# Latent attention with a gated mixture on one Trainium2 core: the attention stage and the combination put into one block

## The chip, the cores and the metric

The kernel runs on one core of one Trainium2 chip. The metric is the device time of one launch in microseconds. Engines are TensorE (PE, PEld for its weight loads), VectorE (DVE), ScalarE (ACT), GpSimd (POOL) and SyncE (SP), which here only issues transfers.

## The reference

The input x has 2048 tokens of width 512. After a layer norm, two branches are computed and multiplied, and x is added:

```python
xn = _layernorm(x)
s = attention(xn)                      # 16 heads, head width 128, rotary width 64, latent width 128
g = silu(ffn(xn))                      # dense 512x512 plus 8 low-rank experts, two of them per token
out = x + s * g
# attention
c_Q = xn @ W_DQ.T;  q = [c_Q @ W_UQ.T , rope(c_Q @ W_QR.T)]
c_KV = xn @ W_DKV.T; k = [c_KV @ W_UK.T, rope(xn @ W_KR.T)];  v = c_KV @ W_UV.T
scores = clip(q @ k.T, -80, 80), causal; weights = softmax(scores / sqrt(192))
s = concat_heads(weights @ v) @ W_O.T
```

All is float32. The kernel splits each factor of a large matmul into a high and a low part (names ending in `_h` and `_l`) and adds three products.

## The kernel before

The kernel has three stages, each a block of its own in which every engine has its own program.

`prepare` normalises x, computes keys, values, latent queries and the linear branch, and stores them in memory (`keys`, `values`, `linear`, `turned`).

`attend` walks over 16 units (`UNITS`), a unit being 256 tokens (`CT`, a couple of tiles) for 8 of the 16 heads. A unit of couple m has 2m + 2 pairs. A pair is a block of 128 keys against the 256 tokens of the unit: the first is the CORNER (causal), the second LATE (only the later 128 tokens), the others FULL. `sweep` calls `pair` on every engine in the same order, 144 pairs in all (`PAIRS`), with hardware loops for the FULL pairs. In a pair TensorE computes scores in two halves (L916 to L928, L946), ScalarE takes the exponential (L1087), VectorE clips (L1177, L1182), ScalarE rounds to the high part (L1093), VectorE adds up the sums (L1190) and subtracts for the low part (L1195), and TensorE weighs the values of the pair before (L968, L987 to L991). Attention outputs stay unnormalised in the latent space; at the end of a unit ScalarE reads them out (L1064), ones times `total` gives the sums (L901), and GpSimd's queue stores both (L831, L833). It also gathers the next unit's rotated queries (L791, L794). SP's queue loads keys (L810) and values (L813) into two slots each.

In unit 15 the corner has no next unit, so no latent queries are computed. Two single transfers on GpSimd's queue bring the weights `wo` (L866, released at 1121.47 by the first half of the scores of unit 15's corner) and `uv` (L869). VectorE inverts the sums of units 0 to 13 in the second FULL pair's end (`early_sums`, L1233), and GpSimd's queue stores them (L871).

`combine` is the third block. TensorE computes the 16 products W_UV times W_O per head into `merge_ps` (L1365), ScalarE and VectorE split them (L1408, L1465), and for each of 16 tiles of 128 tokens the rows of all heads are loaded (L1308), the inverse sums are loaded onto one partition (L1313) and spread by GpSimd (`partition_broadcast`, L1358), VectorE multiplies (L1423), ScalarE takes the high part (L1391), VectorE the low (L1429), and TensorE does 48 matmuls into `sum_ps` (L1376 to L1378). The sigmoid (L1402), the gate product (L1441) and two operations in `finish` (L1447, L1449) follow. Buffers are doubled by the tile's parity. SP also stores the last unit's outputs and sums, loads the late sums (L1333), and stores their inverses (L1335).

The order on each engine is written out by hand with semaphores.

## Time and profile before

| | us |
|---|---|
| median of 3 runs | 1454.61 (1453.51 to 1456.13) |
| profiled execution, its own time | 1453.58 |
| its span, first to last instruction | 1452.1 |
| TensorE busy | 1378.6 (95%) |
| VectorE busy | 1141.7 (79%) |
| ScalarE busy | 781.3 (54%) |
| GpSimd busy | 112.6 (8%) |

The span is what the rows below are placed in; the profiled execution's own time is 1.5 us above its span. Matmul records overlap, so the pitch from start to start, not the duration, is what one costs. TensorE's granted clock averages 0.988 of full speed.

### The profile page before, as it was taken

How to read it: one execution, taken by the hardware profiler on the slowest of the kernel's cores; microseconds unless marked ns; L12 is line 12 of the kernel's file. 1: busy time of each engine (PE TensorE's matmuls, PEld its weight loads, DVE VectorE, ACT ScalarE, POOL GpSimd, SP SyncE). 2: the span in 40 equal slices, each digit the busy share in tenths (PEclk: the TensorE clock that was granted, in tenths of full speed). 3: DMA queues.
4: the chain of work that ended last, by engine and by line, in shares of the span. 5: the costliest groups of instructions: out<-in, count | busy, mean ns of one | idle time of the engine just before them, and what ended most of it. 6: DMA issues, size and time to landing. Idle time of an engine off the chain costs nothing. (4 is left out here: it accounts for less than half of the span.)

```text
span 1452.1 us, 27828 instructions
## 1 busy us (share of the span) xinstructions
PE 1378.6 (95%) x9808; PEld 1133.0 (78%) x9808; DVE 1141.7 (79%) x1322; ACT 781.3 (54%) x854; POOL 112.6 (8%) x150
## 2 busy tenths in 40 slices
PE   5999689999999999999999999999999799599998
PEld 5888567778778888888889888887788688278887
DVE  5666378888888898989888898888788598576764
ACT  3322367666666666666666665666556466332221
POOL 0000111101101101010010100100000000112121
PEclk9999899999999999999999999999999999899999
DMA  6422665535424424242251421422412522345562
GB/s 265 134 90 85 187 187 153 168 130 157 120 89 148 123 85 124 84 126 83 58 152 58 123 87 61 136 74 56 129 54 83 189 57 58 117 132 161 167 181 87
DMA packets 111949, 172.77 MB, mean 119 GB/s; under 512 B 9224, under 2 KB 68904, under 8 KB 109096
## 3 DMA queue, kind: packets, MB, share of 16 engines
q1 hardware_dynamic: 97528, 111.10, 24.8%
q0 software_dynamic: 13552, 59.60, 14.0%
q10 hardware_dynamic: 832, 1.57, 0.5%
q8 instruction: 22, 0.36, 0.1%
q14 instruction: 15, 0.12, 0.0%
HBM read 123.75 MB, written 48.50 MB: 119 GB/s over the span
## 5 line engine op out<-in xcount | busy, mean ns | idle before, releaser
L1093 ACT CAST prob_h<-prob 128x1024 fp32r<-128x1024 f32 (+1 forms) x288 | 289.7, 1006 | 230.4 <-DVE prob L1177 183.1
L946 PE MATMUL score_ps<-q_h,key_slot 64*128 64x512 f32 x1792 | 360.8, 394 | 14.7 <-DMA key_slot<-keys 14.5
L1087 ACT ACTIVATE prob<-score_ps 128x1024 f32<-128x1024 f32 (+1 forms) x288 | 281.8, 978 | 168.0 <-PE score_ps L946 119.0
L1195 DVE TENSOR_TENSOR prob_l<-prob,prob_h 128x1024 fp32r<-128x1024 f32 (+1 forms) x288 | 335.9, 1166 | 39.7 <-ACT prob_h L1093 38.2
L968 PE MATMUL out_ps<-prob_h,value_slot 64*128 64x512 f32 (+1 forms) x1792 | 341.5, 375 | 0.2
L1190 DVE TENSOR_TENSOR total<-total,prob 128x1024 f32<-128x1024 f32 (+1 forms) x256 | 294.9, 1152 | 0.0
L1177 DVE TENSOR_SCALAR prob<-prob 128x1024 f32<-128x1024 f32 x224 | 155.2, 693 | 84.8 <-ACT prob L1087 84.6
L946 PEld LDWEIGHTS score_ps<-q_h,key_slot 64*128 64x128 f32 x1792 | 173.8, 185 | 52.8 <-DMA key_slot<-keys 10.8
L968 PEld LDWEIGHTS out_ps<-prob_h,value_slot 64*128 64x128 f32 x1792 | 173.7, 185 | 33.6 <-DVE prob_l L1195 2.3
L946 PE MATMUL score_ps<-q_l,key_slot 64*128 64x512 f32 x896 | 179.0, 391 | 0.0
L946 PE MATMUL score_ps<-rot_hh,key_slot 64*128 64x512 f32 x896 | 178.9, 390 | 0.0
L968 PE MATMUL out_ps<-prob_l,value_slot 64*128 64x512 f32 (+1 forms) x896 | 172.3, 376 | 0.0
L1391 ACT CAST rows_h<-rows 128x1024 fp32r<-128x1024 f32 x32 | 33.7, 1053 | 128.6 <-DVE rows L1423 127.2
L1376 PE MATMUL sum_ps<-merged_h,rows_h 128*128 128x512 f32 x256 | 100.0, 391 | 0.0
L946 PEld LDWEIGHTS score_ps<-rot_hh,key_slot 64*128 64x128 f32 x896 | 86.7, 184 | 16.9
L1378 PE MATMUL sum_ps<-merged_h,rows_l 128*128 128x512 f32 x256 | 99.6, 389 | 0.0
L1377 PE MATMUL sum_ps<-merged_l,rows_h 128*128 128x512 f32 x256 | 99.6, 389 | 0.0
L968 PEld LDWEIGHTS out_ps<-prob_l,value_slot 64*128 64x128 f32 x896 | 86.9, 185 | 16.1
L946 PEld LDWEIGHTS score_ps<-q_l,key_slot 64*128 64x128 f32 x896 | 86.8, 185 | 12.8
L946 PE MATMUL score_ps<-rot_l,key_slot 64*128 64x512 f32 x448 | 89.4, 390 | 0.0
L1182 DVE SCALAR_TENSOR_TENSOR prob<-prob,causal 128x1024 f32<-128x1024 f32 (+1 forms) x64 | 61.1, 954 | 17.3 <-ACT prob L1087 16.9
L1423 DVE TENSOR_TENSOR rows<-rows,scale 128x1024 f32<-128x1024 f32 x32 | 39.5, 1271 | 31.2 <-POOL scale L1358 31.2
(192 smaller groups left out, 1979.9 us busy)
## 6 DMA issues: line engine op xcount, KB each, us to landing
key_slot<-keys SPq DMA_DIRECT2D x144, 256.0 KB, 2.7
value_slot<-values SPq DMA_DIRECT2D x144, 128.0 KB, 2.0
rows<-heads_rows SPq DMA_DIRECT2D x32, 512.0 KB, 5.8
rot_hh<-turned POOLq DMA_DIRECT2D x30, 512.0 KB, 6.0
heads_rows<-head_rows POOLq DMA_DIRECT2D x15, 1024.0 KB, 10.0
turned<-rot_hl POOLq DMA_DIRECT2D x14, 1024.0 KB, 4.6
rot_l<-turned POOLq DMA_DIRECT2D x30, 256.0 KB, 7.9
wo<-in_w_o POOLq DMA_DIRECT2D x1, 4096.0 KB, 14.5
```

The source lines that it names most:

```text
L946: mm = pe.matmul(score_ps[:, half, c * 512:(c + 1) * 512], keys_of[ROWS[r], :], moving[par][ROWS[r], half * HW + c * 512:half * HW + (c + ...
L968: mm = pe.matmul(out, values_of[ROWS[r], :], moving, start=False, stop=False)
L1087: nc.scalar.activation(prob[half][:, 0:width], score_ps[:, half, 0:width], ACT.Exp, scale=QK_SCALE).then_inc(exp_done, 1)
L1093: nc.scalar.copy(prob_h[half][:, 0:width], prob[half][:, 0:width]).then_inc(high_done, 1)
L1177: nc.vector.tensor_scalar(p, p, P_MIN, P_MAX, ALU.max, ALU.min).then_inc(clipped, 1)
L1182: nc.vector.scalar_tensor_tensor(out=heads, in0=heads, scalar=P_MIN, in1=limit, op0=ALU.max, op1=ALU.min).then_inc(clipped, 1)
L1190: nc.vector.tensor_tensor(sums, sums, by_head(half, kind), ALU.add).then_inc(summed, 1)
L1195: nc.vector.tensor_tensor(p_l, p, p_h, ALU.subtract).then_inc(split, 1)
L1376: pe.matmul(sum_ps[:, par, :], rows_h[par][:, h, :], merged_h[:, h, :], start=(h == 0), stop=False)
L1377: pe.matmul(sum_ps[:, par, :], rows_h[par][:, h, :], merged_l[:, h, :], start=False, stop=False)
L1378: mm = pe.matmul(sum_ps[:, par, :], rows_l[par][:, h, :], merged_h[:, h, :], start=False, stop=(h == HEADS - 1))
L1423: nc.vector.tensor_tensor(rows[par][:, heads, :], rows[par][:, heads, :], scale[par][:, heads, :], ALU.mult).then_inc(scaled, 1)
```

## The change

The blocks `attend` and `combine` become one block, `attend_and_combine`. To make the memory fit, `homes` places buffers of the combination where attention buffers lie whose last use is past. The same edits also move work:

- The weights are loaded in 20 parts by GpSimd's queue, each released by one half pair's scores in unit 13, instead of in two transfers in units 14 and 15.
- The 16 products per head and their split run in the corner pair of unit 15 (on TensorE where other units compute latent queries); the LATE pair's scores wait for the subtractions.
- The inversion of the early sums moves to the same corner, ahead of the split.
- GpSimd's queue, once all 16 products are split, loads rows of tiles 0 and 1 and their scales, the scales spread to all partitions by the transfer. Later tiles are spread by GpSimd as before.
- VectorE multiplies and splits tile 0 in the last four FULL pairs of unit 15 (`closes`), ScalarE copies in two of them; for that the last four pairs of the last couple's units stand outside the loop.
- After the sweep TensorE computes tile 0 (`project(0, 0)`), then the last two weighings and the last sums, then tile 1 and the others. Around it, SP, ScalarE and VectorE have a new order for the first tiles.

The core of the diff:

```diff
                 if not (isinstance(m, int) and m == 1):
-                    with eng.Fori(1, m) as n:
+                    with eng.Fori(1, m - 2 if closing else m) as n:
                         two(t + 2 + 2 * n, unit, 2 * n, FULL)
+                if closing:
+                    two(t + 2 * m - 2, unit, 2 * m - 4, FULL)
+                    two(t + 2 * m, unit, 2 * m - 2, FULL)
...
+        def closes(unit, kind, k, before):
+            return not unit.has_next and kind == FULL and isinstance(k, int) and k == 2 * unit.couple - before
...
             sweep(sp, pair)
+            sp.wait_ge(heads_stored, 16 * (UNITS - 2))
+            sp.wait_ge(inverses_out, 16)
+            load_rows(2, 0)
+            load_scale(2, 0)
+            sp.wait_ge(scored, 2 * PAIRS)
+            load_rest(0, 0)
+            load_rest(1, 1)
+            load_rows(3, 1)
+            load_scale(3, 1)
+            sp.wait_ge(out_read, 2 * UNITS)
+            sp.dma_start(one_of(heads_out, UNITS - 1), head_rows[:, :]).then_inc(last_stored, 16)
+            sp.wait_ge(sums_read, UNITS)
+            sp.dma_start(sums_out[UNITS - 1].rearrange("(q g) t -> q (g t)", g=2), sums[0:P:32, :]).then_inc(last_stored, 16)
...
+            sp.wait_ge(last_stored, 32)
+            sp.dma_start(late_sums, sums_out[EARLY:UNITS].rearrange("u h t -> (u h) t")).then_inc(late_in, 16)
+            for par in range(2):
+                load_rest(2 + par, par)
+                store(par, par)
+            sp.wait_ge(inverted, 2)
+            sp.dma_start(inverses[EARLY:UNITS].rearrange("u h t -> (u h) t"), late_sums).then_inc(late_out, 16)
+            with sp.Fori(1, COUPLES - 2) as n:
+                for par in range(2):
+                    tile(2 * n + par, par)
...
+            pool.wait_ge(passed, 16 * (UNITS - 2))
+            weights = [(wo[h], w_o[:, h, :]) for h in range(HEADS)]
+            for n in range(4):
+                columns = slice(n * 512, (n + 1) * 512)
+                weights.append((uv_flat[:, columns], w_uv[:, columns]))
+            for n, (home, source) in enumerate(weights):
+                pool.wait_ge(scored, 2 * (PAIRS - 4 * COUPLES - 2 * (COUPLES - 1) + 4) + n)
+                pool.dma_start(home, source).then_inc(weights_in, 16)
             during(UNITS - 2, 0, has_second=False)
...
-            pool.wait_ge(scored, 2 * (PAIRS - 2 * COUPLES) + 1)
-            pool.dma_start(top.wo[:, :, :], w_o).then_inc(weights_in, 16)
             during(UNITS - 1, 1, has_next=False, has_second=False)
-            pool.wait_ge(summed_up, UNITS - 1)
-            pool.dma_start(top.uv[:, :, :], w_uv.rearrange("p (h l) -> p h l", h=HEADS)).then_inc(weights_in, 16)
...
+            pool.wait_ge(merge_split, HEADS)
+            pool.wait_ge(summed_up, UNITS - 1)
+            pool.wait_ge(heads_stored, 16 * (UNITS - 2))
+            pool.wait_ge(inverses_out, 16)
+            for par in range(2):
+                for half in range(2):
+                    home, source = rows_of(par, par, half)
+                    pool.dma_start(home, source).then_inc(early_rows, 16)
+                pool.dma_start(scale[par], scale_of(par, par).partition_broadcast(P)).then_inc(early_rows, 16)
...
+                if kind == LATE and not unit.has_next:
+                    pe.wait_ge(merge_split, HEADS - 2)
...
+                        pe.wait_ge(weights_in, 16 * WEIGHT_PARTS)
+                        for h in range(HEADS):
+                            if h % 2 == 0 and h < 4:
+                                pe.wait_ge(exp_done, 2 * t + 1 + h // 2)
+                            since(pe, merge_split, h - 3)
+                            pe.matmul(merge_ps[h % 4], uv[:, h, :], wo[h], start=True, stop=True).then_inc(merged, 1)
...
             sweep(pe, pair)
+            pe.wait_ge(exp_done, 2 * PAIRS - 1)
+            project(0, 0)
             pe.wait_ge(values_in, 16 * PAIRS)
             for half in range(2):
                 weigh(PAIRS - 1, half, 1, FULL, True)
+            pe.wait_ge(summed, 2 * (PAIRS - UNITS))
+            sum_up(1, score_ps[:, 0, DIM:2 * DIM])
             pe.wait_ge(exp_done, 2 * PAIRS)
+            project(1, 1)
+            with pe.Fori(1, COUPLES) as n:
+                for par in range(2):
+                    pe.wait_ge(times[par], n)
+                    project(2 * n + par, par)
...
+                    if closes(unit, kind, k, 3):
+                        high_half(0, 0, 0)
+                    if closes(unit, kind, k, 2):
+                        high_half(0, 0, 1)
...
             sweep(act, pair)
+            high_rows(1, 1, 0)
+            high_rows(2, 0, 1)
             for half in range(2):
                 act.wait_ge(weighed, 2 * PAIRS - 1 + half)
                 read_out(UNITS - 1, half)
+            read_sums(UNITS - 1, score_ps[:, 0, DIM:2 * DIM])
+            gates(0, 0)
+            gates(1, 0)
+            gates(0, 1)
+            high_rows(3, 1, 1)
+            gates(1, 1)
...
+                if closes(unit, kind, k, 4):
+                    dve.wait_ge(early_rows, 16 * EARLY_TILES)
+                    scale_half(0, 0)
+                if closes(unit, kind, k, 3):
+                    scale_half(0, 1)
+                if closes(unit, kind, k, 2):
+                    split_half(0, 0, 0)
+                if closes(unit, kind, k, 1):
+                    split_half(0, 0, 1)
...
+            scale_rows(1, 1, 0)
+            scale_rows(2, 0, 1)
             gates(0, 0)
+            gates(1, 1)
+            finish(0, 0, 0)
+            gates(2, 0)
+            finish(1, 1, 0)
+            dve.wait_ge(late_in, 16)
+            nc.vector.reciprocal(late_sums, late_sums).then_inc(inverted, 1)
```

## Rows read from the trace of the kernel before

**Rows 1.** The page's 40 slices, TensorE's busy tenths.

```profile
PE   5999689999999999999999999999999799599998
```

**Rows 2.** Windows: stretch, its length, busy time of each engine, clock, DMA share, GB/s.

```profile
1140.30:1145.60 5.30, 5.28 (x30) 4.44 (x32) 0.00 (x0) 0.39 (x1) 0.00 (x0) 0.50 0.29 84
1230.60:1237.40 6.80, 6.80 (x62) 5.43 (x58) 6.07 (x7) 4.16 (x5) 0.00 (x0) 1.00 0.07 19
1237.40:1273.95 36.55, 20.55 (x55) 9.26 (x54) 19.12 (x22) 14.83 (x22) 4.48 (x2) 0.81 0.38 117
1273.95:1448.07 174.12, 174.12 (x768) 143.79 (x767) 110.34 (x111) 42.66 (x48) 33.67 (x14) 1.00 0.51 150
```

**Rows 3.** Chain that ended last, between attention and combination: start, length, what.

```profile
1250.59 6.06 DMA scale<-inverses
...
1256.91 1.97 issue
1258.88 2.31 POOL scale L1358
...
1261.29 3.01 DVE rows L1423
...
1264.96 8.99 PE merge_ps L1365 x16
```

**Rows 4.** Timeline of TensorE at the borders of units 14 and 15: start, length, instruction, idle before.

```profile
1027.74 0.50 PE L946 MATMUL score_ps<-q_h,key_slot 64*128 64x512 f32 x2 [1.15 <-DMA key_slot<-keys]
...
1126.08 1.06 PE L901 MATMUL out_ps<-total,ones 128*32 128x512 f32 x8
1128.78 0.47 PE L987 MATMUL out_ps<-prob_h,value_slot 128*128 128x512 f32 x1 [1.63 <-issue]
...
1140.32 0.80 PE L946 MATMUL score_ps<-q_h,key_slot 64*128 64x512 f32 x2 [6.23 <-DMA key_slot<-keys]
```

**Rows 5.** Timeline of ScalarE between attention and combination.

```profile
1245.90 0.58 ACT L1408 CAST merged_h<-merge_ps 128x512 fp32r<-128x512 f32 x1 [1.45 <-PE merge_ps L1365]
1246.76 0.58 ACT L1408 CAST merged_h<-merge_ps 128x512 fp32r<-128x512 f32 x1 [0.27 <-PE merge_ps L1365]
...
1274.59 1.28 ACT L1402 ACT_TABLE_LOAD   x1
```

**Rows 6.** Timeline of VectorE: unit 15's corner, its second full pair, last pair, a tile.

```profile
1128.23 1.23 DVE L1195 TENSOR_TENSOR prob_l<-prob,prob_h 128x1024 fp32r<-128x1024 f32 x1 [1.11 <-ACT prob_h L1093]
...
1158.87 1.75 DVE L1233 RECIPROCAL early_sums<-early_sums 112x256 f32<-112x256 f32 x1
...
1238.06 0.69 DVE L1177 TENSOR_SCALAR prob<-prob 128x1024 f32<-128x1024 f32 x1 [0.27 <-ACT prob L1087]
...
1241.01 1.22 DVE L1190 TENSOR_TENSOR total<-total,prob 128x1024 f32<-128x1024 f32 x1
...
1289.90 2.36 DVE L1423 TENSOR_TENSOR rows<-rows,scale 128x1024 f32<-128x1024 f32 x2 [3.58 <-POOL scale L1358]
1292.25 2.36 DVE L1429 TENSOR_TENSOR rows_l<-rows,rows_h 128x1024 fp32r<-128x1024 f32 x2
```

**Rows 7.** Transfers: KB, median us to landing; landing of keys 1100 to 1160; SP's issues.

```profile
rows<-heads_rows SPq DMA_DIRECT2D x32, 512.0 KB, 5.8
heads_rows<-head_rows POOLq DMA_DIRECT2D x15, 1024.0 KB, 10.0
rot_l<-turned POOLq DMA_DIRECT2D x30, 256.0 KB, 7.9
wo<-in_w_o POOLq DMA_DIRECT2D x1, 4096.0 KB, 14.5
...
DMA to landing us min/median/max: 2.6/2.8/13.7
...
1224.91 0.33 SPq L810 DMA_DIRECT2D key_slot<-keys  x1
...
1280.73 1.42 SPq L1308 DMA_DIRECT2D rows<-heads_rows  x2
```

More of the change, by code:

```diff
@@ L73, in raw, with homes @@
     return ap.bitcast(F32)
+WO_FIRST = 13
+def homes(nc, ctx, side, words, sets):
+    made = []
+    for tensors in sets:
+        with ExitStack() as lent:
+            made.append([lent.enter_context(nc.sbuf_tensor(name, [P, width], dt, side=side)) for name, width, dt in tensors])
+    ctx.enter_context(nc.sbuf_tensor("home_of_" + sets[0][0][0], [P, words], F32, side=side))
+    return made
 class Persistent:
@@ L747, in attend, with by_heads @@
         out_ps = ctx.enter_context(nc.psum_tensor("out_ps", [P, 4, 512], F32))
+        def by_heads(ap, width):
+            return ap.rearrange("p (h n) -> p h n", n=width)
+        wo_parts = [by_heads(keep.wo_first[:, :], DIM), by_heads(wo_rest[:, :], DIM)]
+        wo = [wo_parts[h // WO_FIRST][:, h % WO_FIRST, :] for h in range(HEADS)]
+        uv = by_heads(uv_flat[:, :], LAT)
+        merged_h, merged_l = by_heads(keep.merged_h[:, :], DIM), by_heads(top.merged_l[:, :], DIM)
+        rows, scale, rows_h, rows_l = ([by_heads(ap[:, :], P) for ap in pair] for pair in (
+            (top.rows, rows1), (keep.scale, scale1), (keep.rows_h, rows_h1), (keep.rows_l, rows_l1)))
+        x_in, lin_in, gate = ([ap[:, :] for ap in pair] for pair in (
+            (keep.x_in, keep.x_in1), (lin_in0, lin_in1), (gate0, gate1)))
+        late_sums = late_sums[0:(UNITS - EARLY) * UHEADS, :]
+        result = [sb(f"result{n}", [P, DIM]) for n in range(2)]
+        merge_ps = [score_ps[:, b // 2, (b % 2) * DIM:(b % 2 + 1) * DIM] for b in range(4)]
+        sum_ps = [score_ps[:, par, 0:DIM] for par in range(2)]
         zeroed = sem("zeroed")
@@ L821, in _ @@
+            for par in range(2):
+                store(TILES - 2 + par, par)
+            for par in range(2):
+                sp.wait_ge(stored[par], 16 * COUPLES)
         @block.gpsimd
@@ L1127, in pair, with high_half, high_rows, gates @@
                     latent_high(n + 1, 1 - par, 1)
+                else:
+                    for h in range(HEADS):
+                        act.wait_ge(merged, h + 1)
+                        nc.scalar.copy(merged_h[:, h, :], merge_ps[h % 4]).then_inc(merge_high, 1)
                 begin(1)
+            def high_half(t, par, half):
+                heads = slice(half * UHEADS, (half + 1) * UHEADS)
+                act.wait_ge(scaled, 2 * t + half + 1)
+                nc.scalar.copy(rows_h[par][:, heads, :], rows[par][:, heads, :]).then_inc(rows_high, 1)
+            def high_rows(t, par, n):
+                since(act, projected[par], n)
+                for half in range(2):
+                    high_half(t, par, half)
+            def gates(par, n):
+                act.wait_ge(gate_in[par], 32 * (n + 1))
+                since(act, times[par], n)
+                nc.scalar.activation(gate[par], lin_in[par], ACT.Sigmoid).then_inc(sigmoid, 1)
             gather(act, 0, 0, first_scattered)
@@ L1230, in pair @@
                         split_turned(n)
-                if not unit.has_next and kind == FULL and isinstance(k, int) and k == 1:
-                    dve.wait_ge(early_in, 16)
-                    nc.vector.reciprocal(early_sums[:, :], early_sums[:, :]).then_inc(inverted, 1)
             latent_low(0, 0, 0)
```

331 lines of the change are left out of this document (127 added, 204 removed).

## The prediction

> **What bounds the kernel now.** I read the page first, then the windows by stage, then the chain of waits, and only then single engines around the one weak place. The slices of the page show TensorE at nine tenths or more nearly everywhere, with a visible dent in slice 34 and a small one in slice 31 [rows 1]. The windows say the same in numbers: in one attention pair (1230.6 to 1237.4) TensorE is busy 6.80 of 6.80 us, and in the whole combination (1273.95 to 1448.07) 174.12 of 174.12 us at a granted clock of 1.00 [rows 2]. So in both stages the sum of matmuls sets the time, and nothing but fewer idle stretches of TensorE can be gained.
>
> Between the stages the stretch from 1237.40 to 1273.95 holds 20.55 us of TensorE in 36.55 us [rows 2]. The chain shows what ends late there: a load of the inverse sums (6.06 us), a start of GpSimd (1.97), its broadcast (2.31), VectorE's scaling of tile 0 (3.01), then the rest of the products W_UV times W_O (8.99) [rows 3]. The dent in slice 31 is a load: TensorE sits idle 6.23 us at 1140.32 for a tile of keys [rows 4]. That load took up to 13.7 us instead of 2.8 [rows 7], while the single 4096 KB load of W_O (14.5 us) was under way, and the matmuls that follow run at clock 0.50, which is the 1.2 GHz level [rows 2].
>
> **The change, part by part.** The sum is made on the profiled execution, 1453.58 us in all with a span of 1452.1; the median of the three runs, 1454.61, is 1.0 above it.
>
> 1. The gap closes. After the last pair of the sweep (1237.40) the new order on TensorE is tile 0, the last weighing, the sums, tile 1, and so on. A tile is 174.12 / 16 = 10.88 us [rows 2]. What must still run between 1237.40 and the tiles is two weighings, 12 matmuls at a pitch of 0.23 us = 2.8 us, and the sums, 1.06 us [rows 4]: 3.9 us, the 0.23 being a tile's 10.88 / 48. Before, this stretch took 36.55 us until the first tile. Term: 3.9 - 36.55 = -32.6 us. It holds only if tiles 0 and 1 are prepared in time. Tile 1 is: VectorE's last addition, at 1241.01, ends at 1242.2, and its four operations of a tile take from 1289.90 to 1294.6 in steady state, ScalarE's copies among them, 4.7 us [rows 6], so tile 1 is ready near 1247 and needed at 1237.4 + 10.9 + 3.9 = 1252.2.
>
> 2. The 16 products move into the corner pair of the last unit. They are float32 matmuls, two instructions each, and the pitch of ScalarE's copies, 1245.90 to 1246.76, gives 0.86 us a head [rows 5]. In the old corner the sums start at 1126.08, last 1.06, and TensorE then idles 1.63 us until 1128.78 [rows 4]. New: the first four heads fill the four banks at 1127.15 + 3.4 = 1130.6; head 4 waits for VectorE, which finishes its piece of the pair at 1128.23 + 1.23 = 1129.46, now does the reciprocal (1.75 us [rows 6]) and then the first subtraction, 0.7 us, so 1131.9; twelve more heads, 12 x 0.86 = 10.3, end at 1142.4. The pair goes on there instead of at 1128.78. Term: +13.6 us. Bounds: 12.2 if the wait on VectorE costs nothing (16 x 0.86 - 1.6), 17 if copies and subtractions don't keep the pitch at first. All other work of the corner (ScalarE's 1.0 us copies) lies beside it. The scores after it wait for subtractions 14 and 16, whose last ones end within about 1.5 us of the products, and a weighing of 1.4 us and the first half's scores stand between: nothing.
>
> 3. The weights in 20 parts. 16 parts of 256 KB and 4 of 256 KB, one for each half pair (3.4 us), end before the corner of unit 14. A 256 KB load of keys takes 2.8 us [rows 7], so a part lands within its half pair, and pieces of 2 KB don't stand in front of the keys as rows of 32 KB did. GpSimd's queue waits on each part; behind it stands only the gather for unit 15, released later than the last part. Term: the stall of 6.2 us goes, and with it the low clock: 5.30 us at 0.50 [rows 2] would be 5.30 / 2 = 2.65 at 1.00. -6.2 - 2.6 = -8.8 us. The 1024 KB store of unit 14's rows stays where it is; it and the gathers cost a wait of 1.15 us at the border before [rows 4].
>
> 4. VectorE prepares tile 0 in the last four pairs: two multiplications and two subtractions, about 1.16 us each beyond overlap; ScalarE gets two copies of 1.05. In a pair VectorE is busy 6.07 of 6.80 us [rows 2], so 0.73 is free. Three of the four lie where TensorE still waits for VectorE (the last comes after the last subtraction of the sweep): 3 x 1.16 = 3.5, less the slack of two following pairs (1.5) and about 0.55 that TensorE's weighing lags: +1.5 us. Bounds 0 and 3.5. ScalarE has 4.16 of 6.80 busy [rows 2], so its copies hide. The last subtraction ends near 1243 to 1244 and TensorE wants it for the second half of tile 0 at 1242.9: within the same bounds.
>
> 5. GpSimd's queue loads tiles 0 and 1: four loads of 512 KB and two scales spread over 128 partitions by the DMA itself (1024 KB each). The trace of before has no such spread load. Rows of 512 KB take 5.8 us on SP's queue [rows 7] in 1024 pieces of 512 bytes; a scale has 2048 such pieces, so 11.6. Sum one after another: 4 x 5.8 + 2 x 11.6 = 46 us. Below lies 14.5 us, which W_O's 4096 KB took, above 126 us, by the 256 KB in 7.9 us of the rotated queries on the same queue [rows 7]; those were four loads side by side, so I stay at 46. They start after the 16th subtraction (1143.2) and VectorE wants them in the pair that begins 10 pairs after the late one: 1147.8 + 10 x 6.8 + 6 = 1222, 79 us later. Hidden. Meanwhile they share the engines with the keys, whose load is issued at 1224.91 for a pair that starts at 1230.60, with 5.7 us for 2.8 [rows 7]; I take +1 us in all, 0 to 6.
>
> 6. The start of the combination. Tile 2 reuses the buffers of tile 0, so SP issues it at about 1243.3 (last subtraction of tile 0). In steady state it is 9.2 us from SP's issue (1280.73) to VectorE's multiplication (1289.90) [rows 6, 7]; with up to 2 us for GpSimd's first broadcast, as in the chain [rows 3], tile 2 is multiplied from 1252.5 to 1254.5. ScalarE then copies its two halves (2.2), reads the last outputs and sums (2.6), loads a table (1.28 [rows 5]) and does two sigmoids; VectorE's two gate products and the first product of finish follow. That ends between 1262.3 and 1265.3, and TensorE asks for it (times[0]) at 1263.1: 0 to 2.2 us, I take 1.5. Then late_in: the store of the last rows is issued near 1260, takes 6 to 10 us (1024 KB, median 10.0 [rows 7]), the late sums and reciprocal follow, and the multiplication of tile 3 is queued behind that reciprocal on VectorE; ready at 1275 to 1278.5, needed at 1275.5: 0 to 3, I take 1.5. Tile 4's load is queued behind `inverted` on SP; it just meets its need. Term: +3 us, bounds 0 and 7.
>
> Sum: -32.6 + 13.6 - 8.8 + 1.5 + 1 + 3 = -22.3 us. 1453.6 - 22.3 = 1431.3; by the median of the runs 1432.3. I say 1431.5. No chance of no gain comes out of the terms themselves: +17, +3.5, +6 and +7 all at their bad ends give -32.6 + 17 - 8.8 + 3.5 + 6 + 7 = -7.9 us, 1445.7.
>
> **Rivals.** (a) The first tiles never wait: terms 4 and 6 at their good ends, -4.5 us, 1427 or a little under. For it: the links of the chain in 6 are worth 0 at their short ends. Against: three queues (ScalarE, VectorE, SP) each hold a late link. (b) The chain of the sums takes over: late_in on VectorE holds tile 3, `inverted` on SP holds tile 4, and with a 10 us store and the bad ends of 4 this is +4 to +7: 1436 to 1440. (c) The keys again: the many 512-byte pieces of the six loads hold up the keys of six or seven pairs by 1 to 1.5 us each: 1437 to 1441. For it is the 13.7 us load; against it that the neighbour there had rows of 32 KB. (d) The split does nothing, and some other transfer (the 1024 KB store) made the 13.7 us: term 3 is lost, 1440. Against: the same store at the border before costs 1.15 us [rows 4].
>
> (e) The other side: the six loads are late. VectorE stands at the wait for them ahead of the multiplication in the eleventh full pair, every later piece of attention is queued behind it, and TensorE stops. At the upper bound, 126 us against 79, it is 47 us: 1478. The point from which the kernel is slower is 79 + 22 + 3 = 104 us for the six. For it: descriptors of that queue are made by GpSimd. A mechanism that would do it: VectorE's clip works on 128x1024 in 0.69 us, where its additions need 1.22 [rows 6], and while it runs GpSimd may be shut out; twice 0.69 in 6.80 us is a fifth of the time, which stretches 46 to 58 us and stays under 79. The Trainium skill has this as a rule (SBUF — State Buffer, section on the "DVE blocks DMA" trap): in a two-port mode VectorE holds a port pair alone and GpSimd can't write the descriptors of its transfers. By that rule the loads belong on SP's queue. No row of before shows work held up by it.
>
> **How the numbers follow.** My forecast, 1427 to 1436, has 0.50; (a) under 1427 0.15; (b) 0.16; (c) 0.10; (d) 0.04; (e) 0.05. A measurement of this kernel tells about 0.2%, 3 us. The range 1424 to 1441 takes in (a) to (d) with the bounds of 4, 5 and 6. Faster 0.94, same 0.01, slower 0.05.
>
> **What would show it.** In the profile after: no stretch without TensorE between attention and combination, so slice dents at 31 and 34 gone and one of lower matmul density in the last unit's corner; merge_ps matmuls over some 15 us there at clock 1.00; key loads in the last unit within 5.7 us; early loads landed within about 46 us; waits of sum_ps on VectorE's result of 1 to 2 us at tile 2, and on rows_l at tile 3. It would be wrong if the corner costs more than 17 us, if sum_ps waits more than 7 us in all, or if VectorE's first scaling waits for a DMA.

## The result, and the profile after

The changed kernel takes 1446.45 us (median of 6 runs, 1444.91 to 1448.86) against 1454.06 for the kernel before (6 runs): ratio 0.9955, interval 0.9942 to 0.9967. It is faster, by 7.6 us where 22.3 were forecast, and its time lies 5 us above the range. The profiled execution took 1448.86 us with a span of 1447.4.

The page of the changed kernel, its 40 slices, numbered from 0: the dents in slices 31 and 34 [rows 1] are gone, but slice 35 holds a new one, and the clock has a dent there beside the one early on. A stall around 1158 us lies across slices 31 and 32 and doesn't show.

```profile
PE   4999689999999999999999999999999999979998
...
PEclk9999899999999999999999999999999999989999
```

TensorE's waits, 1000 to 1310 us: what waited and for whom, us in total, times, the longest. One wait of 8.1 us ahead of tile 2 and one of 4.6 us for keys make up most of what is missing from the forecast gain.

```profile
PE score_ps L1218 <- DVE result L1501: 8.1, 1, 8.1
PE score_ps L1103 <- DMA key_slot<-keys: 5.2, 2, 4.6
PE score_ps L1202 <- DVE merged_l L1465: 0.9, 1, 0.9
```

Windows (columns as in [rows 2]): the stall for keys and the stretch behind it, the last pair, the first two tiles with the last weighings and sums between them, the wait ahead of tile 2 and what follows it, and a stretch inside the combination.

```profile
1155.70:1160.30 4.60, 0.02 (x4) 0.01 (x2) 3.94 (x4) 1.77 (x2) 0.00 (x0) 1.00 1.01 372
1160.30:1165.00 4.70, 4.70 (x28) 3.71 (x30) 0.00 (x0) 0.05 (x1) 0.00 (x0) 0.64 0.75 281
1243.90:1250.70 6.80, 6.80 (x60) 6.07 (x56) 6.80 (x8) 4.84 (x5) 0.00 (x0) 1.00 0.08 23
1250.70:1277.20 26.50, 26.50 (x118) 20.33 (x116) 14.53 (x13) 4.51 (x5) 4.48 (x2) 1.00 0.39 119
1277.20:1285.30 8.10, 0.03 (x1) 0.00 (x0) 5.07 (x7) 6.51 (x8) 0.00 (x0) 0.70 0.32 130
1285.30:1291.00 5.70, 5.67 (x14) 4.45 (x15) 1.46 (x3) 0.63 (x1) 0.00 (x0) 0.53 0.50 144
1380.00:1400.00 20.00, 20.00 (x88) 16.27 (x87) 13.88 (x14) 5.48 (x6) 2.30 (x1) 1.00 0.62 184
```

Where 36.55 us held 20.55 of TensorE [rows 2], 26.50 are now full. Both stalls are dearer than they look: after each, the matmuls run for some us for a part at the lower clock level, 1.2 GHz (0.64 and 0.53 in the mean of the windows). In the last stretch 88 matmuls stand where the kernel before has 90 in the same 20 us.

TensorE's timeline in the last unit's corner and at the borders (start, length, instruction, idle before):

```profile
1128.63 1.07 PE L1058 MATMUL out_ps<-total,ones 128*32 128x512 f32 x8
1129.62 3.70 PE L1202 MATMUL score_ps<-wo_first,uv 128*128 128x512 f32 x8
1134.27 7.99 PE L1202 MATMUL score_ps<-wo_first,uv 128*128 128x512 f32 x18 [0.94 <-DVE merged_l L1465]
1142.10 2.74 PE L1202 MATMUL score_ps<-wo_rest,uv 128*128 128x512 f32 x6
1144.27 0.80 PE L1144 MATMUL out_ps<-prob_h,value_slot 128*128 128x512 f32 x1
...
1285.33 0.79 PE L1218 MATMUL score_ps<-merged_h,rows_h 128*128 128x512 f32 x1 [8.11 <-DVE result L1501]
```

The trace files `merge_ps` and `sum_ps` under `score_ps`, which holds them all now, so L1202 is the products and L1218 to L1220 are the tiles. From the sums to the next weighing it is 15.64 us, against 2.70 in [rows 4].

The wait ahead of tile 2, followed back. First VectorE and ScalarE:

```profile
1273.78 4.15 DVE L1419 TENSOR_TENSOR rows<-rows,scale 128x1024 f32<-128x1024 f32 x2 [11.97 <-POOL scale L1009]
...
1283.29 1.29 DVE L1495 TENSOR_TENSOR gate<-gate,lin_in 128x512 f32<-128x512 f32 x2 [2.97 <-ACT gate L1337]
1284.50 0.68 DVE L1501 TENSOR_TENSOR result<-score_ps,gate 128x512 f32<-128x512 f32 x1
```

```profile
1276.88 2.13 ACT L1326 CAST rows_h<-rows 128x1024 fp32r<-128x1024 f32 x2 [16.33 <-DVE rows L1419]
1278.91 1.92 ACT L1249 COPY head_rows<-out_ps 128x1024 f32<-128x1024 f32 x2
1280.72 0.60 ACT L1256 COPY sums<-score_ps 128x512 f32<-128x512 f32 x1
1281.34 1.28 ACT L1337 ACT_TABLE_LOAD   x1
```

Then GpSimd's broadcast by its line, with the marks of its sequencer; the first mark of a pass of the loop stands where the broadcast is released, in later passes 0.1 us ahead of its start (count, duration, first and last start):

```profile
L1009 POOLq MODIFY_POOL_CONFIG  x14: 11/11/11, 1263.1 to 1409.7; - x14
L1009 POOL PARTITION_BROADCAST scale<-scale x14: 2297/2297/2509, 1271.4 to 1421.1; - x14
```

The scale was there and the broadcast released at 1263.1; it began at 1271.4, 8.3 us later. Of the others, 12 begin when their scale lands and one right behind the first. VectorE had stood 11.97 us, and its two multiplications then took 4.15 us instead of 2.36, while GpSimd was spreading the second scale. The kernel before has the same start: the marks of its first broadcast are at 1252.3 and 1258.9, so 6.6 us. Its chain shows only 1.97 us of "issue" [rows 3]: the chain merges the first two broadcasts and follows the load of the second scale, which covers most of the start.

### The profile page after: what moved, and what is told of

Read it like the earlier page. It is cut to its first block, busy times and chain, and to the rows that moved or that the text cites. A ratio compares the mean times of both kernels' runs of the same rounds, so it can differ in the third digit from the quotient of the medians.

```text
span 1447.4 us, 27577 instructions
## 1 busy us (share of the span) xinstructions
PE 1384.2 (96%) x9808; PEld 1135.4 (78%) x9808; DVE 1143.9 (79%) x1322; ACT 780.9 (54%) x854; POOL 122.2 (8%) x172
## 4 chain that ended last, share of the span: by engine, by line
PE 74%; DMA 6%; DVE 5%; ACT 1%; issue 1%; SPq 0%; POOL 0%; POOLq 0%; DVEq 0%; ACTq 0%
PE score_ps L1103 29%; PE out_ps L1125 18%; DMA key_slot<-keys 5%; PE score_ps L1219 4%; PE score_ps L1218 4%; PE score_ps L1220 4%; PE out_ps L1144 2%; PE out_ps L1145 2%; PE out_ps L1148 2%; PE score_ps L1073 1%; PE score_ps L1074 1%; PE score_ps L1075 1%; PE score_ps L1076 1%; DVE prob_l L1415 1%; PE score_ps L1038 1%
## 5 line engine op out<-in xcount | busy, mean ns | idle before, releaser
L1103 PE MATMUL score_ps<-q_h,key_slot 64*128 64x512 f32 x1792 | 360.5, 393 | 10.8 <-DMA key_slot<-keys 10.7
L1218 PE MATMUL score_ps<-merged_h,rows_h 128*128 128x512 f32 x256 | 102.0, 399 | 8.1 <-DVE result L1501 8.1
L1219 PE MATMUL score_ps<-merged_l,rows_h 128*128 128x512 f32 x256 | 102.0, 399 | 0.0
L1220 PE MATMUL score_ps<-merged_h,rows_l 128*128 128x512 f32 x256 | 101.3, 396 | 0.0
L1218 PEld LDWEIGHTS score_ps<-merged_h,rows_h 128*128 128x128 f32 x256 | 48.9, 191 | 21.3 <-issue 9.7
```

Source lines behind the costliest of these rows:

```text
L1103: mm = pe.matmul(score_ps[:, half, c * 512:(c + 1) * 512], keys_of[ROWS[r], :], moving[par][ROWS[r], half * HW + c * 512:half * HW + (c + ...
L1218: pe.matmul(sum_ps[par], rows_h[par][:, h, :], merged_h[:, h, :], start=(h == 0), stop=False)
L1219: pe.matmul(sum_ps[par], rows_h[par][:, h, :], merged_l[:, h, :], start=False, stop=False)
L1220: mm = pe.matmul(sum_ps[par], rows_l[par][:, h, :], merged_h[:, h, :], start=False, stop=(h == HEADS - 1))
```

## The experiments

My theory after the result: the first broadcast of the program starts some 8 us late and is 8 of the missing us (with the low clock behind it 10.7); the burst of six loads makes the 4.6 us for keys. Rivals: the order on ScalarE (tile 2's copies ahead of the gates) makes the late sigmoid anyway; the keys are late by the place of their own slot, not by the burst; the 256 KB parts are not what cured the weights; and the place of buffers, or of the PSUM banks, or the clock, makes the slower pitch. Kernels that were not timed side by side are compared by their ratios to the kernel before, times 1453 us, the others by their medians; an interval of such a ratio is some 2 us to either side.

**First broadcast early.** GpSimd does one small broadcast of its own after the six loads.

```diff
+            nc.gpsimd.memset(ready_tile[:, :], 0.0).then_inc(ready, 1)
+            pool.wait_ge(ready, 1)
+            nc.gpsimd.partition_broadcast(ready_tile[:, :], ready_tile[0:1, :], channels=P).then_inc(ready, 1)
+            pool.wait_ge(ready, 2)
```

> The changed kernel, and GpSimd runs one partition broadcast of 8 elements right after it has issued the six early loads, about 115 us before the first real one. Theory (the first broadcast on GpSimd takes about 8 us from its release to its start, and this makes tile 2 late): the first real broadcast starts under 1 us after its scale has landed, TensorE's wait of 8.1 us ahead of tile 2 falls to 0 to 2 us and the low clock behind it goes with it, so 8 to 11 us less than the changed kernel: ratio to the kernel before 0.987 to 0.990. Rival 1 (the wait for the scale's transfer or for the loop of the queue sets the start): the start stays 8 us after landing, ratio 0.9955. Rival 2 (ScalarE's order of read-outs and gates sets tile 2): the broadcast comes early, but the wait stays over 5 us.

1437.74 us, ratio 0.9893 (0.9877 to 0.9909), 9 us under the changed kernel. GpSimd's timeline:

```profile
1161.98 0.28 POOL L1026 PARTITION_BROADCAST ready_tile<-ready_tile  x1 [9.43 <-issue]
1264.29 2.30 POOL L1011 PARTITION_BROADCAST scale<-scale  x1 [102.03 <-DMA scale<-inverses]
1269.82 2.65 POOL L1011 PARTITION_BROADCAST scale<-scale  x1 [3.23 <-DMA scale<-inverses]
```

An instruction of 0.28 us began 9.3 us after its release (mark at 1152.7); the one of 2.30 us began when its scale landed. TensorE has no wait ahead of tile 2, and its wait for keys is unchanged at 5.1.

**Loads paced.** Each of the six loads waits for one more pair of unit 15.

```diff
+            for n, (home, source) in enumerate(early):
+                pool.wait_ge(scored, 2 * (PAIRS - 2 * COUPLES + 3 + n) + 1)
+                pool.dma_start(home, source).then_inc(early_rows, 16)
```

> The changed kernel, but each of the six early loads on GpSimd's queue waits for the first half scores of one further full pair instead of all going out at once. Theory (the burst of six loads, 4 MB, holds up the keys of the second full pair: landing 9.9 us instead of 2.7): no key load in the last unit over 5.5 us, no wait of TensorE there, and the stretch at low clock behind it gone: 5 to 6 us less than the changed kernel, ratio 0.9915 to 0.992. Rival (any single load of 512-byte pieces holds keys up, whatever is queued behind it): several key loads of 4 to 6 us, several waits of 1 us, and nothing gained. Rival 2: the instructions unrolled in the last unit cause the wait: it stays at 4.6 us.

1439.53 us, 0.9912 (0.9894 to 0.9930), 6 us under the changed kernel. TensorE waits 0.9 us for keys, and tile 2 still waits:

```profile
PE score_ps L1220 <- DVE result L1503: 7.4, 1, 7.4
PE score_ps L1105 <- DMA key_slot<-keys: 0.9, 1, 0.9
```

So the two waits are independent, and the burst is what made the second.

**Early scales spread by GpSimd.** The scales go to one partition, ahead of the rows, and are spread by two broadcasts, which both halves the bytes of the burst and moves the first broadcast.

```diff
-                pool.dma_start(scale[par], scale_of(par, par).partition_broadcast(P)).then_inc(early_rows, 16)
+                pool.dma_start(scale[par][0:1, :, :], scale_of(par, par).unsqueeze(0)).then_inc(early_scale, 16)
...
+            pool.wait_ge(early_scale, 32)
+            for par in range(2):
+                nc.gpsimd.partition_broadcast(scale[par], scale[par][0:1, :, :], channels=P).then_inc(early_spread, 1)
```

> The changed kernel, but the scales of tiles 0 and 1 are loaded onto one partition (8 KB each) and spread by GpSimd's broadcast in the last unit, as for the other tiles; four loads of 512 KB remain on the queue. It removes 2 MB of the 4 MB burst and moves the first broadcast far ahead of tile 2. Theory: both waits shrink. Ahead of tile 2 0 to 2 us instead of 8.1; the key load lands after 6 to 7 us instead of 9.9, so a wait of 1 to 2 us instead of 4.6. Together 11 to 14 us less than the changed kernel: 0.985 to 0.988. If the two broadcasts hold VectorE up in the last unit, up to 2 us of it is lost. Rival (size of the burst does not matter, one packet of the other queue in front of each packet does): the wait for keys stays at 4 to 5 us.

1435.51 us, 0.9888 (0.9871 to 0.9905), 10 us under the changed kernel where 11 to 14 were expected. TensorE waits 2.8 us for keys and 0.6 ahead of tile 2. With 2 MB of rows instead of 4 MB in all, the worst key load took 8.1 us instead of 9.9.

**Gates before tile 2.** ScalarE's and VectorE's work on tile 2 moves behind the gates of tiles 0 and 1; the broadcast stays as late as it was.

```diff
-            high_rows(2, 0, 1)
             for half in range(2):
...
             gates(1, 0)
+            high_rows(2, 0, 1)
             gates(0, 1)
```

> The changed kernel with another order in the hand-over: ScalarE reads the last outputs and sums and computes the gates of tiles 0 and 1 before it copies tile 2, and VectorE finishes tile 0 before it multiplies tile 2. Nothing else is changed, the first broadcast stays late. Theory: tile 2 then waits only for its own rows, which are ready near 3 to 4 us after TensorE has ended tile 1; the wait falls from 8.1 to 3 to 4 us, and the clock loss behind it to under 2: 5 us less, ratio 0.992. Rival (the chain through result and gates is only named last and the rows are as late): wait 7 us or more, ratio 0.995.

1438.31 us, 0.9905 (0.9889 to 0.9920), 7 us under, with a wait of only 1.0 on `rows_l` where I had expected 3 to 4. The late start is the cause, but it needs the order to do harm: in the changed kernel the sigmoid of tile 0 is queued behind the copies of tile 2. Here the first product of `finish` ends at 1266.8, 7 us before TensorE has done with tile 1, and tile 2's own rows, though the broadcast still began 7.1 us after its release, are only 1.0 us late.

**The kernel before with the weights in parts**, released by the scores of unit 15's pairs; nothing else changed.

```diff
+            for n, (home, source) in enumerate(parts):
+                pool.wait_ge(scored, 2 * (PAIRS - 2 * COUPLES) + 4 + n)
+                pool.dma_start(home, source).then_inc(weights_in, 16)
```

> The kernel before, with one part of the change alone: the weights in 20 parts of 256 KB, each released by one more half pair of the last unit; blocks, products and tiles stay as before. Theory (the 13.7 us key load was held up by the single 4096 KB load with its 32 KB rows): the wait of 6.2 us at the first full pair of the last unit goes, and the 2.6 us of low clock behind it, 8.8 us less: ratio 0.994. Rival (the 1024 KB store of the last outputs and the border itself hold the keys up): ratio 0.999 to 1, key landing still over 8 us.

1445.52 against 1454.14 on the same chip, 0.9951 (0.9937 to 0.9966): -8.6 us, where the term said -8.8. TensorE waits 0.9 us in all for keys instead of 6.2 and 1.2 [rows 4], and the gap before the combination is much as it was (12.3 us of waiting for `merged_l`, 13.1 before). The first part is issued at 1133.45, where the single load was at 1121.47, so this shows what the whole term is worth and not what the size alone is.

**Weights in three loads**, at the same place in unit 13 of the changed kernel.

```diff
+            weights = [(wo_parts[0], w_o[:, 0:WO_FIRST, :]), (wo_parts[1], w_o[:, WO_FIRST:HEADS, :]), (uv_flat[:, :], w_uv)]
...
+                pool.wait_ge(scored, 2 * (PAIRS - 4 * COUPLES - 2 * (COUPLES - 1) + 4) + 6 * n)
```

> The changed kernel with the weights in three transfers (3328, 768 and 1024 KB) in place of 20, from the same point on, 20 us apart. Theory (long rows on the other queue hold up keys): a key load of 10 us or more in unit 13 and a wait of 3 to 8 us of TensorE with a stretch of low clock, 5 to 9 us more than the changed kernel: ratio 0.999 to 1.002. Rival (in the middle of a unit keys have enough time): no wait over 1 us, ratio 0.9955 or a little less.

1448.03 us, 0.9961 (0.9946 to 0.9976), 1 to 3 us over the changed kernel's two ratios (0.9955 and, further down, 0.9943) and not clear of them, where 5 to 9 were expected. The dump of 3328 KB took 10.8 us and the worst key load beside it 7.2, which cost TensorE 1.5 us:

```profile
PE score_ps L1100 <- DMA key_slot<-keys: 1.6, 2, 1.5
```

So the place is worth most of the 8.8 us. It isn't that keys have more slack in mid-unit: a landing of 7.2 us left a wait of 1.5 there, so 5.7 were covered, and 13.7 left 6.2 in the kernel before, so 7.5 were. The delay itself was shorter. In the kernel before the store of unit 14's rows (1024 KB) and `uv` (1024 KB) were under way together with the 4096 KB; which of them made the difference was not tried.

**Three remedies together**: scales spread by GpSimd, the four row loads paced, and the early reciprocal behind the 16 subtractions instead of ahead of them.

```diff
-                        dve.wait_ge(early_in, 16)
-                        nc.vector.reciprocal(early_sums[:, :], early_sums[:, :]).then_inc(inverted, 1)
                         for h in range(HEADS):
...
+                        dve.wait_ge(early_in, 16)
+                        nc.vector.reciprocal(early_sums[:, :], early_sums[:, :]).then_inc(inverted, 1)
```

> The changed kernel with the scales of tiles 0 and 1 loaded onto one partition and spread by GpSimd, the four early row loads one per full pair, and the inversion of the early sums after the 16 subtractions in place of before them. Theory: no wait of TensorE over 1 us is left in the last unit nor ahead of tile 2, and the corner is 0.9 us shorter. 5.9 + 11.0 + 0.9 us less than the changed kernel, less up to 2 us for VectorE held up by the broadcasts: 16 to 18 us, ratio 0.983 to 0.985. Rival (a new late link takes the place of those removed, as tile 3 behind the late sums): ratio 0.987 to 0.989 with a wait of 3 us or more ahead of tile 3 or 4.

1431.64 us, 0.9854 (0.9840 to 0.9868), 15 us under the changed kernel. The waits on keys are down to 0.7 and those ahead of tiles are gone, but a new one stands in the pairs. VectorE's timeline while GpSimd spreads two scales in attention:

```profile
1153.64 1.22 DVE L1414 TENSOR_TENSOR total<-total,prob 128x1024 f32<-128x1024 f32 x1
1154.84 3.12 DVE L1419 TENSOR_TENSOR prob_l<-prob,prob_h 128x1024 fp32r<-128x1024 f32 x1
1157.88 2.78 DVE L1401 TENSOR_SCALAR prob<-prob 128x1024 f32<-128x1024 f32 x1
1160.59 1.21 DVE L1414 TENSOR_TENSOR total<-total,prob 128x1024 f32<-128x1024 f32 x1
```

1.2 and 0.69 us became 3.12 and 2.78, and TensorE waited 2.5 us.

**Tile 0 prepared after the sweep**: the multiplications, copies and subtractions of tile 0 leave the last four pairs.

```diff
-                if closes(unit, kind, k, 4):
-                    dve.wait_ge(early_rows, 16 * EARLY_TILES)
-                    scale_half(0, 0)
...
+            dve.wait_ge(early_rows, 16 * EARLY_TILES)
+            for half in range(2):
+                scale_half(0, half)
+            for half in range(2):
+                split_half(0, 0, half)
             scale_rows(1, 1, 0)
```

> The changed kernel without VectorE's part: tile 0 is multiplied and split after the last addition of attention, not in the last four pairs; ScalarE's two copies move too. Theory (the gap between the stages closes only because tile 0 is ready at the end of the sweep): TensorE waits 6 to 8 us ahead of tile 0, tile 2's loads start later too, so its wait stays near 8 us; the pairs are under 1 us faster. 7 to 10 us more than the changed kernel: ratio 1.000 to 1.003. Rival (tile 0's late start is taken back by a shorter wait ahead of tile 2): ratio 0.9955 to 0.998.

1447.83 us, 0.9962 (0.9948 to 0.9976): only 1 to 3 us over the changed kernel's two ratios, where 7 to 10 were expected. The waits show why:

```profile
PE score_ps L1218 <- DVE rows_l L1423: 9.5, 2, 8.2
...
PE score_ps L1218 <- DVE result L1490: 0.2, 1, 0.2
```

The wait moved from tile 2 to tile 0: the first broadcast began at 1271.21, as late as in the changed kernel, so TensorE did its idling earlier and asked for tile 2 later.

**The same with the three remedies in place.**

> The kernel of e7 (scales of tiles 0 and 1 spread by GpSimd, row loads paced, inversion after the subtractions), but tile 0 is multiplied and split after the last addition, as in e8. Theory (in e8 nothing was lost because the late tile 2 took the wait over; with the first broadcast early it no longer does): TensorE waits about 8 us ahead of tile 0 and loses 2 to 3 us at low clock, 8 to 10 us more than e7: ratio 0.991 to 0.992. Rival (preparing tile 0 in the last pairs is worth nothing in itself): ratio 0.986, wait under 3 us.

1441.58 us, 0.9921 (0.9906 to 0.9937). Against 0.9854 this is 10 us: tile 0 waits 8.2 us for `rows_l` and nothing comes back later. VectorE's part of the change is worth 10 us, and in the changed kernel the late broadcast takes most of it.

**The kernel before with the first broadcast early**, the same four lines as in the first experiment, at the head of the combination.

> The kernel before with one addition: at the start of the combination's program GpSimd runs one partition broadcast of 8 elements, while the loads of tile 0 are on their way. Theory (the first broadcast's 6.6 us from release to start is a cost of its being the first): the broadcast of tile 0 starts within 1 us of its scale's landing, and the chain up to tile 0 is 5 to 7 us shorter: ratio 0.9955 to 0.9965. Rival (the scale's transfer or the second scale's landing is what it waits for): start unchanged, ratio 0.999 to 1.001.

1447.49 against 1453.13 on the same chip, 0.9959 (0.9944 to 0.9974): -5.6 us. The single wait of TensorE among the first products, for `merged_l`, is 4.9 us instead of 13.1.

```profile
1250.86 0.28 POOL L1355 PARTITION_BROADCAST ready_tile<-ready_tile  x1 [7.02 <-issue]
1251.53 2.30 POOL L1364 PARTITION_BROADCAST scale<-scale  x1 [0.39 <-POOL ready_tile L1355]
```

The release mark is at 1244.0, 6.9 us ahead of the small broadcast. The late start was in the kernel before, too, and the chain had shown 1.97 us of it.

**All remedies without a broadcast in the way**: first broadcast early on the small tile, all six loads paced and spread by the transfer, reciprocal behind the subtractions.

> The changed kernel with e1 and e2 together (all six early loads stay loads, one per full pair; a broadcast of 8 elements behind them) and the inversion of the early sums after the 16 subtractions. Theory (the two waits are independent and add up, and no broadcast meets VectorE in the last unit as in e7): 5.9 + 11 + 0.9 us less than the changed kernel, 0 to 2 us under e7: ratio 0.984 to 0.986. Rival (one of them hid the other, the gains don't add): 0.988 or more.

1430.78 us, 0.9843 (0.9827 to 0.9859); the changed kernel beside it, 1445.59. From 1110 us to the end of the matmuls the trace has one wait of TensorE:

```profile
PE score_ps L1227 <- DVE rows_l L1434: 0.2, 1, 0.2
```

**The changed kernel again.**

> The changed kernel as it is, on the same chip as the others of this call, as a measure for differences of 1 to 2 us: ratio 0.9945 to 0.9965, wait ahead of tile 2 near 8 us and for keys near 4.6 us as before. If these waits differed from run to run by some us, the single profiles would not carry the reading.

1445.59 us, 0.9943 (0.9926 to 0.9959). Its two waits, 6.9 and 4.8 us, are those of the first profile. The one ahead of tile 2 is 1.2 us shorter, and so is the start of the first broadcast (1262.3 to 1269.3, 7.0 us).

**`merged_l` and the second homes change sides.** Where the changed kernel has `merged_l` in the right half of the memory and `rows_h1`, `rows_l1` in the left, they are exchanged, and with them the attention buffers whose place they take (even and odd units' queries).

```diff
-            (("merged_l", HEADS * DIM, F32R),)))
+            (("rows_h1", HQ, F32R), ("rows_l1", HQ, F32R), ("lin_in1", DIM, F32), ("gate1", DIM, F32), ("late_sums", CT, F32))))
...
-        q_h, q_l, rot_hh, rot_l0 = [top.q_h, q_h1], [top.q_l, q_l1], [top.rot_hh, rot_hh1], [top.rot_l0, rot_l01]
+        q_h, q_l, rot_hh, rot_l0 = [q_h1, top.q_h], [q_l1, top.q_l], [rot_hh1, top.rot_hh], [rot_l01, top.rot_l0]
```

> The changed kernel with two homes swapped and nothing else: the queries of even units and, after them, merged_l lie at the left side of SBUF, those of odd units and, after them, rows_h1, rows_l1, lin_in1, gate1 and late_sums at the right. Theory (matmuls whose moving data lie at the right side, in turn with others at the left, follow each other more slowly): the combination goes back to 226 to 228 ns, even units become fast and odd ones slow, and the whole is about 3 us less than the changed kernel (16 tiles x 48 x 4.5 ns = 3.5 us, less what unit 15 loses by being slow, 14 pairs x 30 x 5 ns = 2 us, plus what unit 14 gains): ratio 0.992 to 0.994. Rival (PSUM banks 0 and 2 for sum_ps in place of 4 and 5 set the pitch): 231 ns as before, ratio unchanged at 0.9945 to 0.9955.

1445.57 us, 0.9951 (0.9934 to 0.9967): no gain, where 0.992 to 0.994 was expected. The mechanism shows all the same. Windows of 20 us in the middle of units 14 and 15, first of the kernel before, then of this one:

```profile
1060.00:1080.00 20.00, 20.00 (x176) 16.16 (x174) 17.87 (x18) 11.64 (x12) 0.00 (x0) 1.00 0.20 59
1180.00:1200.00 20.00, 20.00 (x178) 16.51 (x178) 17.92 (x18) 12.07 (x13) 0.00 (x0) 1.00 0.22 59
1380.00:1400.00 20.00, 20.00 (x90) 16.57 (x89) 13.06 (x14) 4.75 (x5) 4.59 (x2) 1.00 0.59 175
```

```profile
1060.00:1080.00 20.00, 20.00 (x180) 16.52 (x178) 17.85 (x18) 12.31 (x12) 0.00 (x0) 1.00 0.20 57
1180.00:1200.00 20.00, 20.00 (x174) 17.30 (x173) 17.33 (x19) 11.69 (x12) 0.00 (x0) 1.00 0.18 59
```

At clock 1.00 and with TensorE always busy, the even unit was the slow one (176 against 178 records) and is now the fast one (180 against 174). For attention only the places of the two sets of queries were exchanged. Read from start to start of matmuls that follow each other, it is 232.5 and 226.7 ns before, 226.7 and 232.4 here. In the combination the pitch is 226.7 ns in all tiles of the kernel before, 231.2 in the changed kernel, and 228.9 (even tiles) and 231.2 (odd) here. The theory had 226 to 228 for all of them. The attention units only trade places, so little of a gain was to be had.

**The same exchange on top of the remedies**, with the remedies alone beside it.

> The kernel of e11 with the homes swapped as in e13. Theory: 3 us under e11, ratio 0.9815 to 0.983, tiles at 226 to 228 ns a matmul. Rival (PSUM banks): as e11, 0.984 to 0.985.

> The kernel of e11 once more, for the difference to e14 on the same chip: ratio 0.983 to 0.986, 231 ns a matmul in the combination, no wait of TensorE over 1 us from unit 15 on.

1428.89 us, 0.9838 (0.9820 to 0.9856), and 1431.01 us, 0.9857 (0.9836 to 0.9879). Both beat both kernels; the 2.1 us between them lie within the intervals, and the exchanged one missed its 0.9815 to 0.983, its tiles being at 229.0 (even) and 231.3 ns (odd). It has the lowest median of all versions, 24 us under the kernel before.

## Why the forecast failed, step by step

The forecast's terms beside what the profile of the changed kernel measures for each, us:

| term | forecast | measured | from |
|---|---|---|---|
| 1, gap | -32.6 | -31.8 | 26.5 us for two tiles and 3.9 of other work, 25.7 forecast |
| 2, products in the corner | +13.6 | +12.9 | 15.64 against 2.70 |
| 3, weights in parts | -8.8 | -8.8 | no wait and no low clock left at unit 15's first FULL pair; -8.6 alone in its experiment |
| 4, VectorE prepares tile 0 | +1.5 | +0.3 | 13 pairs in 90.4 us less 1.7 of low clock, 88.4 at 6.80 each |
| 5, early loads | +1 | +6.3 | 4.6 wait, 1.7 low clock (11 pitches in 4.22 us, 2.49 at full clock) |
| 6, start of the combination | +3 | +10.7 | 8.1 wait, 2.6 low clock ahead of tile 2; nothing at tiles 3 and 4 |
| pitch in the combination | 0 | +3.0 | 14 x 48 x (231.2 - 226.7) ns, tiles 0 and 1 being in term 1 |
| sum | -22.3 | -7.4 | |

The two profiled executions differ by 4.7 us, the medians by 7.6. From the sums at the head of unit 15's corner (1126.08 before, 1128.63 after) to the end of the span it is 326.0 and 318.8 us, 7.2 us less, where the table adds up to 7.4. Ahead of the corner the changed kernel is 2.55 us later, and that is scatter: in the other profile of the same kernel the sums start at 1127.56, and in nine profiles of variants that differ from it only behind this place, at 1122.2 to 1128.7.

**Steps 1 to 4 held**, each within 1.2 us. (In step 2 the forecast's own addends end at 1142.2, not 1142.4, so +13.4.) Step 4 was the least certain and came out free: VectorE is busy 6.80 of 6.80 us in the last pair, and TensorE never waits for it there. All its slack is used and none more was needed.

**Step 6 failed, and with it the forecast.** It came out at +10.7 us for +3, above its own bound of 7, and the sign that the prediction named, over 7 us of waiting of `sum_ps`, appeared (8.1). It is a mis-sized term: "up to 2 us for GpSimd's first broadcast, as in the chain". The forecast put the multiplication of tile 2 between 15.1 and 17.1 us after the end of the last pair; it came at 1273.78 - 1250.84 = 22.9. The start alone is 6.3 us longer than the bound allowed (8.3 for 2); the rest up to there came 0.5 us sooner. Another 1.8 is the second broadcast, which VectorE meets now since the two scales wait side by side. The rest of the chain in step 6, its order and within about a us its length, was right: copies, last outputs, table load, sigmoids, gate product, first product of `finish`. Moving the broadcast's start (-9 us) removes the wait and changing the order (-7 us) leaves 1.0 us of it, and together with the 5.6 us in the kernel before this settles it. The GPSIMD Engine Reference of the Trainium skill states such a cost for the first call of a freshly loaded GpSimd kernel (section on instruction dispatch, about 6 us). The 5.8 to 9.3 us measured over all profiles here, from the release of the first broadcast to its start, agree in kind and reach further.

**Step 5 was mis-sized as well**, 6.3 us for 1 and just above its bound of 6. The six loads did not run one after another in 46 us; the last had landed at about 1164.5, 18 us after the first was issued (1146.47), and the DMA engines were busy throughout (a share of 1.01 in the stall's window). Landing of the rows and scales in 1148 to 1165, median us:

```profile
scale<-inverses POOLq DMA_DIRECT2D x2, 1024.0 KB, 11.5
rows<-heads_rows POOLq DMA_DIRECT2D x3, 512.0 KB, 10.3
```

In that stretch the longest key load took 9.9 us. The harm is one large delay in the unit's second FULL pair, not small ones in many pairs, as rival (c) had it: from 1165 to 1245 no key load took over 3.0 us. Rival (c) had the size, 5.5 to 9.5 us over the forecast where pacing the loads takes 6 off, and the wrong place.

**The rivals.** (a) fell in the changed kernel, but the repaired versions lie at 1429 to 1431.6, on the forecast's 1431.5: the structure is worth about what was said once its two stalls are gone. By the table, -7.4 less the 10.7, the 6.3 and the corner's wait of 0.9 makes -25.3; the version with all remedies measures -22.4 against the kernel before. That this is the very number forecast is partly luck: the forecast had 5.5 us of losses in steps 4 to 6, while the repaired version has almost none of them and loses 3 us to the pitch, which the forecast had at nothing. (b) fell: tiles 3 and 4 never wait for late sums. (d) fell by the experiment on the kernel before. Its cousin, that the size of the parts matters little, held: three loads cost 1 to 3 us more than twenty, which is not clear of noise. (e) fell: the loads were there 69 us before VectorE's first multiplication of tile 0 (1233.57). The changed kernel is no test of the mechanism in (e), since the burst was issued by 1152.4, ahead of the unit's first full-width clip (1153.66). The paced loads are one: with VectorE busy 45.06 of 50.00 us and a clip in every half pair, rows landed in 4.6 us and scales in 7.5 (medians). The rule weighed there, from the page "SBUF — State Buffer" of the Trainium skill (the "DVE blocks DMA" trap), would have had GpSimd's queue held up by such clips if they run in its two-port mode; these landings show no sign of it. What did hold is contention the other way round: VectorE's 128x1024 operations stretch while GpSimd spreads a scale (4.15 for 2.36 us, 3.12 for 1.22).

**A term was missing**: the pitch. The forecast took the tile's 10.88 us over unchanged, though buffers moved. The exchange shows for the attention units that the place of the operands sets it. In the combination it moved the even tiles alone, from 231.2 to 228.9 ns and not back to 226.7, so there the place is a part, and the other rival, the PSUM banks, was not tried. Which pairs of places cost and why stays open.

## What to carry to other kernels

When a chain shows an engine's first use of an instruction as a short "issue", look at the release of that very instruction: here the chain showed 1.97 us of a start of 6.6. A burst of loads costs what it delays the one load that comes due while it lasts (9.9 us of landing, 5.3 of them covered), so pace it and keep it away from other large transfers; the size of its parts mattered little. And a gain behind a stall is not additive: VectorE's preparation was worth 1 to 3 us with the late broadcast in place and 10 us without it. One profile places a wait, but not the total: the time up to unit 15's corner alone differed by up to 6.5 us between profiles of kernels that are the same up to there.

## What the runs showed of the hardware

- The first broadcast of the program begins 5.8 to 9.3 us after its release in 17 profiles; the first of each later pass starts 0.1 us after its mark. A broadcast of 8 elements (0.28 us) ahead of time hides it. GpSimd's first `affine_select`, in the first microseconds of the program, idles 8.1 to 12.2 us before it starts, 11.40 and 9.25 in the two profiles of the changed kernel.
- The pitch of 512-column matmuls at clock 1.00 is 226.7 ns with one set of the queries' buffers and 232.4 with the other, and goes with the buffers when they are exchanged. In the combination it is 226.7 to 231.3 ns in different versions, where the place in SBUF is a part of it and the rest open.
- While GpSimd spread a scale, VectorE's operations took up to four times their length (0.69 us became 2.78, 1.22 became 3.12); while the transfers spread the same data (1148 to 1160 of the changed kernel) these operations took their usual 0.69 and 1.22 us.
- After the stalls of 4.6 and 8.1 us TensorE's granted clock was at the 1.2 GHz level for some us, which lost 1.7 and 2.6 us more, about a third on top of the wait. The 6.2 us in the kernel before cost 2.6 more.
